# DLRM tower with a compressed interaction network on one core: rows ordered by dimension, first copies from three queues, weight loads after them

## What is computed

```python
x0 = xk = e
for W in (f0, f1, f2):            # (39*39, 128), (128*39, 128), (128*39, 128)
    z = einsum('bfd,bgd->bfgd', x0, xk).reshape(b, f*g, d)
    xk = einsum('bpd,pm->bmd', z, W)
    outs.append(xk)
z = concatenate(outs, axis=1).sum(-1)          # 1024 x 384
h = relu(concatenate([z, dense_ctx], 1) @ W_top1 + b_top1)
h = relu(h @ W_top2 + b_top2)
y = h @ W_top3
```

## Time and profile before

| | us |
|---|---|
| median of 3 runs | 1467.61 (1467.0 to 1467.76) |
| the profiled execution, its own time | 1464.04 |
| its span, first to last instruction | 1462.3 |
| mean granted TensorE clock in it | 0.971 |

### The profile page before, as it was taken

One profiled execution on the slowest core, in us unless ns is written; L12 is line 12 of the kernel. 1 busy time (PEld: TensorE's weight loads), 2 busy tenths in 40 slices (PEclk: granted clock), 3 DMA queues, 4 the chain that ended last, 5 costly groups with the idle time before them and its releaser, 6 DMA issues.

```text
span 1462.3 us, 20057 instructions
## 1 busy us (share of the span) xinstructions
PE 1344.7 (92%) x5856; PEld 1001.8 (69%) x5856; DVE 1212.5 (83%) x2792; ACT 907.2 (62%) x3233; POOL 676.1 (46%) x666
## 2 busy tenths in 40 slices
PE   0059999999999999999999999999999998988998
PEld 0036676667777777777777777777777676766677
DVE  0249999998989999899889989898989989898874
ACT  0226776666666676667666676666766665655563
POOL 6737656554445555554545547354545423123200
PEclk8579999999999999999999999999999999999999
DMA  7131212120300212010210202101210202010000
GB/s 181 35 109 29 66 45 69 27 65 3 92 27 21 66 50 63 27 52 16 80 33 27 65 21 85 34 26 42 73 40 27 64 1 94 21 38 24 1 1 1
DMA packets 54456, 67.28 MB, mean 46 GB/s; under 512 B 13927, under 2 KB 25945, under 8 KB 54346
## 3 DMA queue, kind: packets, MB, share of 16 engines
q1 hardware_dynamic: 36811, 59.70, 12.9%
q0 software_dynamic: 9984, 2.58, 1.6%
q10 hardware_dynamic: 7551, 3.72, 1.0%
HBM read 10.02 MB, written 0.00 MB: 7 GB/s over the span
## 4 chain that ended last, share of the span: by engine, by line
PE 69%; DVE 17%; issue 5%; ACT 5%; ACTq 2%; another core or an unknown queue 1%; DMA 0%; SPq 0%; DVEq 0%
PE Y L707 16%; PE Y L709 14%; PE Y L708 14%; PE C L655 9%; PE C L669 5%; PE S L663 5%; DVE sum_b L572 4%; ACT Y L436 4%; DVE cur L596 4%; DVE sum_a L572 3%; DVE Y L593 2%; DVE part L585 2%; ACTq L227 2%; PE S L629 1%
## 5 line engine op out<-in xcount | busy, mean ns | idle before, releaser
L436 ACT ACTIVATE Y<-Y,x_col 128x128 f32<-128x128 f32 x2944 | 800.8, 356 | 447.2 <-PE Y L709 415.9
L707 PE MATMUL Y<-f_high,cur_high 128*128 128x512 f32 (+1 forms) x1280 | 627.6, 490 | 32.2 <-DVE cur L596 23.2
L709 PE MATMUL Y<-f_high,cur_low 128*128 128x512 f32 (+1 forms) x1280 | 500.1, 391 | 0.0
L708 PE MATMUL Y<-f_low,cur_high 128*128 128x512 f32 (+1 forms) x1280 | 499.6, 390 | 0.0
L347 POOL TENSOR_TENSOR pairs<-shifted,base 117x512 f32<-117x512 f32 x186 | 241.0, 1296 | 548.5 <-PE C L655 546.6
L572 DVE SCALAR_TENSOR_TENSOR sum_a<-Y,x_col,sum_a 128x128 f32<-128x128 f32 x1024 | 349.6, 341 | 13.9 <-issue 0.5
L707 PEld LDWEIGHTS Y<-f_high,cur_high 128*128 128x128 f32 x1280 | 242.4, 189 | 171.0 <-DVE cur L596 57.9
L320 POOL DMA_INDIRECT rows<-in_tbl_dram,ids_sb x312 | 304.1, 975 | 72.4 <-issue 58.9
L572 DVE SCALAR_TENSOR_TENSOR sum_b<-Y,x_col,sum_b 128x128 f32<-128x128 f32 x896 | 305.1, 341 | 0.5 <-DVE sum_a L572 0.4
L708 PEld LDWEIGHTS Y<-f_low,cur_high 128*128 128x128 f32 x1280 | 243.1, 190 | 84.9 <-issue 47.4
L709 PEld LDWEIGHTS Y<-f_high,cur_low 128*128 128x128 f32 x1280 | 241.5, 189 | 51.7
(11 more groups left out here) (73 smaller groups left out, 554.6 us busy)
## 6 DMA issues: line engine op xcount, KB each, us to landing
shifted<-x_seq SPq DMA_DIRECT2D x157, 234.0 KB
base<-x_seq SPq DMA_DIRECT2D x96, 78.0 KB
rows<-in_tbl_dram,ids_sb POOLq DMA_INDIRECT x312
shifted<-x_seq SPq DMA_DIRECT2D x32, 156.0 KB
rows<-rows SPq DMA_DIRECT2D x14, 312.0 KB
G<-in_L_rec_f_dram ACTq DMA_DIRECT2D x3, 832.0 KB
w_sb<-in_W_top_dram SPq DMA_DIRECT2D x1, 768.0 KB
shifted<-x_seq ACTq DMA_DIRECT2D x3, 234.0 KB
```

The costliest lines, as they stand in the source:

```text
L436: ins = act.activation(where[:, i * M:(i + 1) * M], where[:, i * M:(i + 1) * M], ACT.Copy, scale=x_col[:, t // JT % QG, t % JT, f:f + 1])
L707: pe.matmul(where, ch, wh, start=True, stop=False)
L708: pe.matmul(where, ch, wl, start=False, stop=False)
L709: pe.matmul(where, cl, wh, start=False, stop=True).then_inc(y_filled, 1)
```

## The change

- `rows` has one buffer of 39 features. A new tile `rows_seq` holds 16 dimensions of 123 features, in this order, so that PE's transposes read their weights contiguously.
- For step 0 the four parts of it are copied by ACT (features 0 to 38), DVE (39 to 77 and the last 6) and POOL (78 to 116). In the loop POOL copies all four, in the third and fourth tile of each step's second group (`take_rows`), ahead of the pairs of these tiles; SP's three DMAs go.
- Gathers of a step take 14 tiles instead of 16; none are issued in the two tiles with the copies.
- Group 0's copies are issued by three queues: SP base 0, 1 and shifted 2, 4; ACT base 2 and shifted 1, 3; POOL shifted 5, 6. POOL issues 4 of step 1's early gathers before them and 12 after them.
- f2, w1 and w2 are loaded by SP after the copies of group 1. ACT issues the mirrored f0 after its part of the f1 split; DVE makes f0_sum first and f1_low after its copies of step 0.

```diff
+ROW_PARTS = [(0, NF), (NF, NF), (2 * NF, NF), (SEL, SEQ - SEL)]
...
+FIRST_EARLY = 4
...
-    step, u = divmod(t + AHEAD, TPB)
-    if step == 0:
+    if t < TPB - AHEAD:
         n, tiles = NF - EARLY, TPB - AHEAD
         return 1, range(EARLY + n * t // tiles, EARLY + n * (t + 1) // tiles)
-    if step + 1 >= BT:
+    step, u = divmod(t + AHEAD, TPB)
+    u, tiles = u - 2, TPB - 2
+    if step + 1 >= BT or u < 0:
         return None
-    return step + 1, range(NF * u // TPB, NF * (u + 1) // TPB)
+    return step + 1, range(NF * u // tiles, NF * (u + 1) // tiles)
...
-        rows = sb("rows", [P, 2, SEQ * D])
+        rows = sb("rows", [P, NF * D])
+        rows_seq = sb("rows_seq", [P, D, SEQ])
...
-        gathered = [sem("gathered_even"), sem("gathered_odd")]
+        gathered = sem("gathered")
...
-        first_repeat, repeated, x_read = sem("first_repeat"), sem("repeated"), sem("x_read")
+        first_rows, rows_taken, x_read = sem("first_rows"), sem("rows_taken"), sem("x_read")
...
+        pool_copied = sem("pool_copied")
...
+        by_dim = rows[:].rearrange("p (f d) -> p d f", d=D)
+
+        def row_part(lo, n):
+
+            return rows_seq[:, :, lo:lo + n], by_dim[:, :, 0:n]
+
         def base_copy(eng, g, j):
...
+        POOL_COPIES = (5, 6)
+
         def shift_copy(eng, g, k):
+            done = pool_copied if g == 0 and k in POOL_COPIES else copied[k - 1]
             cols = x_cols(*divmod(g, QG))
             r = K0_ROWS[k]
-            eng.dma_start(shifted[0:r, k - 1, :], cols[k:k + r, :]).then_inc(copied[k - 1], 16)
+            eng.dma_start(shifted[0:r, k - 1, :], cols[k:k + r, :]).then_inc(done, 16)
...
             load_f0(sp, False)
-            sp.dma_start(f2_sb[:], f2.rearrange("(f g) m -> g f m", g=M)).then_inc(f2_in, 16)
-            sp.dma_start(w1_sb[:], w1[0:3 * P, :].rearrange("(k p) n -> p k n", p=P)).then_inc(mlp_in, 16)
-            sp.dma_start(w1_dense[:], w1[3 * P:3 * P + D, :]).then_inc(mlp_in, 16)
-            sp.dma_start(w2_sb[:], w2.rearrange("(k p) n -> p k n", p=P)).then_inc(mlp_in, 16)
-
             sp.wait_ge(first_read, 4)
-            for j in range(BLK):
+            for j in (0, 1):
                 base_copy(sp, 0, j)
-            for k in (2, 4, 6):
+            for k in (2, 4):
                 shift_copy(sp, 0, k)
...
                     shift_copy(sp, g, k)
-                if q == 2 and bt + 1 < BT:
-                    sp.wait_ge(gathered[(bt + 1) % 2], 16 * NF * ((bt + 1) // 2 + 1))
-                    for lo, n in ((NF, NF), (2 * NF, NF), (SEL, SEQ - SEL)):
-                        r = rows[:, (bt + 1) % 2, :]
-                        sp.dma_start(r[:, lo * D:(lo + n) * D], r[:, 0:n * D]).then_inc(repeated, 16)
                 if g == 1:
+                    sp.dma_start(f2_sb[:], f2.rearrange("(f g) m -> g f m", g=M)).then_inc(f2_in, 16)
+                    sp.dma_start(w1_sb[:], w1[0:3 * P, :].rearrange("(k p) n -> p k n", p=P)).then_inc(mlp_in, 16)
+                    sp.dma_start(w1_dense[:], w1[3 * P:3 * P + D, :]).then_inc(mlp_in, 16)
+                    sp.dma_start(w2_sb[:], w2.rearrange("(k p) n -> p k n", p=P)).then_inc(mlp_in, 16)
                     sp.dma_start(b1_sb[:], b1.rearrange("(m p) -> p m", p=P),
...
                     pool.indirect_dma_start(
-                        out=rows[:, bt % 2, f * D:(f + 1) * D], out_offset=None, in_=tables[f],
+                        out=rows[:, f * D:(f + 1) * D], out_offset=None, in_=tables[f],
                         in_offset=bass.IndirectOffsetOnAxis(ap=ids_sb[:, bt, f:f + 1], axis=0),
-                    ).then_inc(gathered[bt % 2], 16)
+                    ).then_inc(gathered, 16)
+
+            def take_rows(bt, j):
+
+                if j == 0:
+                    pool.wait_ge(gathered, 16 * NF * (bt + 1))
+                    if bt > 1:
+                        pool.wait_ge(s_filled, S_USE["x", bt - 1, JT - 1] + 1)
+                    else:
+                        pool.wait_ge(first_filled, 4)
+                lo, n = ROW_PARTS[j]
+                pool.tensor_copy(*row_part(lo, n)).then_inc(rows_taken, 1)
...
                 else:
-                    pool.wait_ge(copied[k - 1], 16 * (g + 1))
+                    pool.wait_ge(copied[k - 1], 16 * (g if k in POOL_COPIES else g + 1))
                     shift = shifted[0:r, k - 1, :]
...
             gather(0, range(NF))
-            gather(1, range(EARLY))
+            pool.wait_ge(gathered, 16 * NF)
+            pool.tensor_copy(*row_part(2 * NF, NF)).then_inc(first_rows, 1)
+            pool.wait_ge(first_rows, 4)
+            gather(1, range(FIRST_EARLY))
+            pool.wait_ge(first_read, 4)
+            for k in POOL_COPIES:
+                shift_copy(pool, 0, k)
+            gather(1, range(FIRST_EARLY, EARLY))
             pool.wait_ge(ones_set, 1)
...
                     fs = list(now[1]) if now else []
-                    if now and now[0] == 2 and now[1][0] == 0:
-                        pool.wait_ge(first_filled, 4)
-                    elif now and now[0] > 2 and now[1][0] == 0:
-                        pool.wait_ge(s_filled, S_USE["x", now[0] - 2, JT - 1] + 1)
+                    if now and now[0] > 1 and now[1][0] == 0:
+                        pool.wait_ge(rows_taken, len(ROW_PARTS) * (now[0] - 1))
+                    if q == 1 and j >= 2 and bt + 1 < BT:
+                        for part in ((0, 1), (2, 3))[j - 2]:
+                            take_rows(bt + 1, part)
                     ks = ((0, 1, 2), (3, 4), (5, 6), ())[j] if g + 1 < NG else ()
...
             act.dma_start(dense_sb, dense.rearrange("(t p) c -> p t c", p=P)).then_inc(dense_in, 16)
-            load_f0(act, True)
             lo = 0
...
                 lo = hi
+            load_f0(act, True)
             for h in range(2):
...
-            act.wait_ge(gathered[0], 16 * NF)
-            act.activation(rows[:, 0, NF * D:2 * NF * D], rows[:, 0, 0:NF * D], ACT.Copy).then_inc(first_repeat, 1)
+            act.wait_ge(gathered, 16 * NF)
+            act.activation(*row_part(0, NF), ACT.Copy).then_inc(first_rows, 1)
             for i in (0, 2):
...
             act.wait_ge(first_read, 4)
-            for k in (1, 3, 5):
+            base_copy(act, 0, 2)
+            for k in (1, 3):
                 shift_copy(act, 0, k)
...
             dve.memset(x_col[:, :, :, NF:FC], 1.0).then_inc(ones_set, 1)
+            dve.wait_ge(f0_in, 16 * len(pieces))
+            dve.wait_ge(mirror_zero, 1)
+            n = K0 - 1
+            dve.tensor_tensor(f0_sum[:, 0:n, :], f0_sum[:, 0:n, :], f0_mirror[:, 0:n, :], ALU.add).then_inc(f0_ready, 1)
+            r = K0_ROWS[n]
+            dve.tensor_tensor(f0_sum[0:r, n, :], f0_sum[0:r, n, :], f0_mirror[0:r, n, :], ALU.add).then_inc(f0_ready, 1)
+
+            dve.wait_ge(gathered, 16 * NF)
+            dve.tensor_copy(*row_part(NF, NF)).then_inc(first_rows, 1)
+            dve.tensor_copy(*row_part(SEL, SEQ - SEL)).then_inc(first_rows, 1)
+            for i in (1, 3):
+                dve.wait_ge(first_filled, i + 1)
+                dve.tensor_copy(x_seq[:, 0, 0:GB, 4 * i:4 * i + 4],
+                                Y[0:SEQ, 512 * i:512 * (i + 1)].rearrange("p (d b) -> p b d", d=4)[:, 0:GB, :])\
+                   .then_inc(first_read, 1)
             lo = 0
...
                 else:
-                    dve.wait_ge(copied[k - 1], 16)
+                    if k in POOL_COPIES:
+                        dve.wait_ge(pool_copied, 16 * len(POOL_COPIES))
+                    else:
+                        dve.wait_ge(copied[k - 1], 16)
                     shift = shifted[0:r, k - 1, :]
...
-            def x_rows(bt, d):
-                return rows[:, bt % 2, :].rearrange("p (f d) -> p d f", d=D)[:, d, :]
-
             def s_free(use):
...
                 s_free(("x", bt, i))
-                pe.wait_ge(repeated, 48 * bt)
+                pe.wait_ge(rows_taken, len(ROW_PARTS) * bt)
                 for n in range(4):
-                    ins = pe.transpose(S[0:SEQ, n * P:(n + 1) * P], x_rows(bt, 4 * i + n), ident[:])
+                    ins = pe.transpose(S[0:SEQ, n * P:(n + 1) * P], rows_seq[:, 4 * i + n, :], ident[:])
                 ins.then_inc(s_filled, 1)
...
-            pe.wait_ge(first_repeat, 3)
+            pe.wait_ge(first_rows, 4)
             for i in range(4):
                 for n in range(4):
-                    ins = pe.transpose(Y[0:SEQ, 512 * i + n * P:512 * i + (n + 1) * P], x_rows(0, 4 * i + n), ident[:])
+                    ins = pe.transpose(Y[0:SEQ, 512 * i + n * P:512 * i + (n + 1) * P], rows_seq[:, 4 * i + n, :], ident[:])
                 ins.then_inc(first_filled, 1)
...
             pe.wait_ge(f0_ready, 2)
```

14 lines of the change are left out of this document (removed).

## The result

The kernel after took 1469.65 us in the median of 15 runs (1465.7 to 1473.3), the kernel before 1466.77 beside it (15 runs, 1464.8 to 1469.1). The ratio is 1.0020, with a 95% interval of 1.0010 to 1.0029: no gain, and a loss of about 0.2%, which is just what a measurement can tell. The forecast was 1446.

What follows compares the result with a forecast made beforehand. The prediction took the loop to be bound by PE, DVE close behind. It summed 1464.04 -2 -15.7 -1.1 -4.5 +1.5 = 1442.2, against the median 1446 us; own range 1438 to 1454, 8-in-10 range 1438 to 1503.

Steps and rivals of the forecast that it cites:

- Start, to the first transposes: Stretch before PE's first transposes: they start at 58.5 instead of 60.46, -2 us (bounds -4 to +3).
- the rival: "f0 is late": ACT's f0 issues bound the start, 5 us later, 1451 us; chance 0.41 together with the forecast.
- The late copies: Third and fourth x_seq copy out of PSUM at the start: contiguous weights and fewer gathers make them timely, -15.7 us (0 to -15.7).
- From there to the first chunk: Base copies' issue to the first pair at the start: shorter issue from three queues, -1.1 us (0 to -1.5).
- The loop: Steps after the start: transposes' weight loads shrink (-4.5 us), POOL's row copies hold up DVE (+1.5 us).
- -4.5: Transposes' weight loads in the loop: contiguous reads are shorter, a third of 12.8 us counted (bounds 0 to -12.8).
- +1.5: POOL's row copies in the loop: DVE's L593 waits 0.7 us a group, with small changes at other places +1.5 us.
- The lock-out rival: Second tile's L593 waits out POOL's whole unbroken run in six groups: 57 us, kernel at 1501 or 1517; chance 0.37.
- It all cancels: Whole kernel: a partial lock-out against the start's gain, within 0.2% of 1467.6 us; chance 0.05.

Runs made afterwards that it cites:

- gathers_pace: Kernel after with two buffers for the gathered rows, so gathers keep the pace of the kernel before (39 over 16 tiles); GpSimd's loop copies stay: 1440.88 us, ratio 0.9951.
- before_again: The kernel before, unchanged, run again on an occasion of the 1448 us kind: 1448.01 us, ratio 1.000.
- after_again: The kernel after, unchanged, run again on an occasion where the kernel before took about 1448 us: 1458.81 us, ratio 1.0069.
- before_third: The kernel before, unchanged, run once more on an occasion of the slow kind: 1466.94 us, beside 1468.59.

## Why the prediction was wrong

- **Start, to the first transposes (-2).** +2.3 in the first comparison, inside the bounds; -0.6 on the other occasion (58.12 to 57.51). ScalarE's f0 issues bound it, as the rival said.
- **The late copies (-15.7).** Right in the first comparison: 19.35 to 3.60 us behind the first transpose, -15.7. But it was luck that the first comparison met such an occasion: on the other kind there is nothing to gain, and the one profile of the kernel before could not tell.
- **From there to the first chunk (-1.1).** 17.7 us before (79.81 to 97.48), 17.2 after (66.38 to 83.61): -0.4.
- **The loop: this step failed.** It was -4.5 +1.5 = -3.0, and the 31 groups took 22.8 us more (13.4 on the other occasion). Both terms were too small. The weights gave -7.5 in the groups with transposes instead of -4.5, inside the bounds, and the 13 us in which they stand are not taken apart; the copies cost +4.7 (2 to 10) instead of +1.5. With the two alone the step is right in sign and near in size: gathers_pace has 4.4 us less in its 31 groups than before_again. What was missing is a term. The diff also puts 39 gathers into 14 tiles instead of 16. The prediction names the two emptied tiles only in a rival, for the length of GpSimd's run, and puts the gathers' new pace at nothing, without a reason. It is +17.9 in the kernel after and +22.0 alone.
- **The parts together**, on the 1448 occasions, each kernel against the one ahead of it: start +0.9, ordered weights and what goes with them -13.0, copies +4.7, pace +17.9, in all +10.5 for the +10.7 measured. That it comes out is no proof of the parts: the steps lead from before to after, so they must add up, and pace alone cost 22.0 and not 17.9. In the first comparison the start's -13.9 stands against this, and group 0 (+3.9) and group 1 (+4.8) lost more than on the other occasion (+1.0 and +2.9).
- **The lock-out rival** had the mechanism and the wrong place. It priced 57 us for one L593 in each of six groups; in group 9 that one lost 0.6 us. The mechanism took its time at other sums, about half of it in groups in which the change has no step, by moving GpSimd's spreads and pairs 1.7 us against them.
- **"It all cancels"**, with a chance of 0.05, is the rival that came true: a partial lock-out against the start's gain, 0.14% from 1467.6. It gave neither the place nor the size of that lock-out.
- The rule of the Trainium skill (SBUF — State Buffer, Who interferes with whom) that a VectorE instruction with two SBUF inputs contends with a GpSimd instruction that reads SBUF fits the rows shown here. The prediction took the wait to be one instruction long. The page says "for the whole instruction" of VectorE's two-port modes, and here it is longer: L618 met four spreads and a pair (3.95), L594 two pairs and four spreads (4.80). The measurement decides: the wait can last until GpSimd leaves a gap. In none of the twenty traces did a sum wait across a pause of GpSimd of 0.14 us or more, and none that came in a pause lasted over 0.4 us.

## What to carry to other kernels

Cost every schedule number in a diff, also one that only spreads the same work over fewer tiles: here it cost more than any part that the change was made for. Where VectorE reads two operands from SBUF, ask of each such instruction which GpSimd instruction it meets and when the next gap comes; if GpSimd has pauses to spare, a gap between its long instructions can pay (23 to 25 us here), and one too many can cost (10 us here). And before a stall is priced as won, see it in a second profile of the same kernel, taken at another time and on another chip.

## What the runs showed of the hardware

**TensorE's clock after a pause.** Groups 9 and 13 of the kernel after run the same program. PE waits 1.92 us before a chunk in one and 1.86 in the other; windows of the stretch behind (PEclk is the third number from the end):

```profile
494.60:499.30 4.70, 4.66 (x13) 3.59 (x14) 4.59 (x12) 2.59 (x9) 1.02 (x1) 0.66 0.01 2
664.50:669.30 4.80, 4.72 (x23) 3.82 (x24) 4.70 (x13) 2.95 (x11) 1.07 (x1) 1.00 0.02 2
```

Behind the pause of 1.92 us the granted clock was 0.66 over 4.7 us, part of it at the lower of its two levels (1.2 GHz for 2.4), and the group took 42.8 us; the other stayed at 1.00 and took 41.3. The length of the pause does not decide it: in after_again a pause of 2.02 us in group 9 left the clock at 1.00 (41.4 us), and one of 1.89 in group 13 was followed by 0.64 over 4.7 us (42.8). So the same small lock-out of VectorE costs 1.5 us of PE on top of itself in some groups and nothing in others.

**Two kinds of occasion.** The same instructions, 47 to 49 small copies issued by ScalarE, took 22.16 us in before_again, 40.73 in the first comparison and 46.02 in before_third.

**A wait in the loop.** In group 0 of the kernel after ScalarE waited 2.16 us for an L737, until 119.42. Six gathers had run one behind the other from 110.7 to 117.9, and GpSimd's spread followed them. The wait is part of that group's 3.9 us; whether PE's signal came late there is not shown.
